# A two-layer graph kernel: one gathered piece in 64 is fetched by SyncE row by row instead of by GpSimd

## The reference

```python
h = relu(layernorm(x))
xW  = einsum('nd,rde->nre', h, W_rel)               # 8 products per node: a table of 100,000 rows of 128
agg = segment_sum(xW[src, edge_type], dst)          # first gather, 212,500 rows of 512 bytes
h2  = gelu(layernorm(agg + h @ W_self + b_conv))    # then a dense feed-forward part
x   = x + (h + h2) + ff(h + h2)
g   = relu(layernorm(x))
xt  = g @ W.T + bias                                # plus 4 source scores per node: a table of rows of 132
alpha = leaky_relu(alpha_src[src] + alpha_dst[dst])
w     = exp(alpha - segment_max(alpha, dst)[dst])
out   = x + segment_sum(xt[src] * w, dst) / segment_sum(w, dst)   # second gather, rows of 528 bytes
```

## Time and profile before

| | us |
|---|---|
| runs | 6048.98, 6045.95, 5961.02 |
| median | 6045.95 |
| span of the profiled execution | 4509.7 |
| median less that span | 1536.3 |
| POOL busy, of the span | 3197.0 |
| indirect transfers of the first and of the second stage | 1680 and 1664 |

### The profile page before, as it was taken

The page is one execution under the profiler, slowest core; times in us unless marked ns, Lnnn a source line. Parts: engine busy times, 40 slices in busy tenths (PEclk is TensorE's granted clock), DMA queues, the critical chain, the costliest instruction groups (busy, mean ns, idle before and its releaser), DMA issues.

```text
span 4509.7 us, 47117 instructions
## 1 busy us (share of the span) xinstructions
PE 2498.0 (55%) x13797; PEld 2093.8 (46%) x13902; DVE 2470.8 (55%) x6772; ACT 962.3 (21%) x3200; POOL 3197.0 (71%) x3372
## 2 busy tenths in 40 slices
PE   7823444444444444444444666666666666666665
PEld 3423343433434333343333556555555565555555
DVE  6741333333333333333334777777777777777777
ACT  4500111111111111111122222222222222222222
POOL 1077777777777777777756777777777777777774
PEclk9966766667667666666666787777777777777777
DMA  8712222222222222222213222222222222222221
GB/s 281 273 50 53 58 62 58 62 58 60 60 58 62 58 60 60 58 62 58 60 43 107 55 57 60 57 57 60 57 60 57 58 60 57 60 57 59 58 57 44
DMA packets 170560, 314.19 MB, mean 70 GB/s; under 512 B 58980, under 2 KB 100108, under 8 KB 169615
## 3 DMA queue, kind: packets, MB, share of 16 engines
q0 software_dynamic: 107008, 222.77, 20.6%
q1 hardware_dynamic: 47810, 81.58, 5.1%
q10 hardware_dynamic: 15490, 6.87, 0.6%
HBM read 239.51 MB, written 71.49 MB: 69 GB/s over the span
## 4 chain that ended last, share of the span: by engine, by line
POOL 68%; issue 23%; PE 6%; DVE 2%; ACT 0%; DMA 0%; POOLq 0%; DVEq 0%; ACTq 0%; SPq 0%
POOL G L512 68%; PE quad L1440 1%; PE quad L1441 1%; PE bank L1440 1%; PE bank L1441 1%; PE bank L1482 0%; PE quad L1511 0%; PE quad L1517 0%; ACT A L663 0%; POOLq L111 0%; PE quad L1434 0%; PE quad L1506 0%; DMA x_res<-in_x 0%; DMA xt_table<-w_all 0%; PE bank L1434 0%
## 5 line engine op out<-in xcount | busy, mean ns | idle before, releaser
L512 POOL DMA_INDIRECT G<-rel_table,idx x1680 | 1601.5, 953 | 705.6 <-issue 511.2
L512 POOL DMA_INDIRECT G<-xt_table,idx x1664 | 1574.6, 946 | 543.8 <-issue 543.8
L1602 PEld LDWEIGHTS quad<-ident,top 128*128 128x128 f32 x3328 | 591.1, 279 | 265.6 <-issue 265.5
L1602 PE MATMUL quad<-ident,top 128*128 128x128 f32 x3328 | 607.6, 367 | 177.5 <-DVEq L1238 177.5
L1025 DVE SCALAR_TENSOR_TENSOR agg<-bank,sel,agg 128x128 f32 x208 | 63.6, 347 | 1093.0 <-PE bank L1482 1091.6
L1633 PE MATMUL bank<-M,onehot 128*128 128x132 f32 x3328 | 432.7, 284 | 149.8 <-DVE M L1287 145.4
L1482 PE MATMUL bank<-G,onehot 128*128 128x128 f32 x1664 | 271.6, 340 | 401.3 <-DMA G<-rel_table,idx 397.0
L1633 PEld LDWEIGHTS bank<-M,onehot 128*128 128x128 f32 x3328 | 398.5, 193 | 181.6 <-issue 181.6
L1482 PEld LDWEIGHTS bank<-G,onehot 128*128 128x128 f32 x1664 | 267.6, 256 | 406.0 <-issue 406.0
L1618 PE MATMUL bank<-Z,w_all 128*128 128x8 f32 x832 | 160.5, 321 | 380.3 <-issue 374.4
L768 ACT ACTIVATE M<-G,M 128x32 f32<-128x32 f32 x1664 | 363.9, 308 | 13.6 <-ACT M L763 0.4
(11 more groups left out here) (320 smaller groups left out, 3530.9 us busy)
## 6 DMA issues: line engine op xcount, KB each, us to landing
rel_table<-G SPq DMA_DIRECT2D x98, 512.0 KB, 3.1
G<-rel_table,idx POOLq DMA_INDIRECT x1680, 2.5
G<-xt_table,idx POOLq DMA_INDIRECT x1664, 7.1
xt_table<-w_all SPq DMA_DIRECT2D x25, 264.0 KB, 3.2
x_mid<-X SPq DMA_DIRECT2D x25, 256.0 KB, 2.0
out<-A SPq DMA_DIRECT2D x24, 256.0 KB
x_res<-in_x ACTq DMA_DIRECT2D x12, 448.0 KB, 5.0
x_res<-x_mid SPq DMA_DIRECT2D x3, 1792.0 KB, 15.5
```

The lines of the kernel that those rows point to most:

```text
L512: g.indirect_dma_start(out=G[:, s, c, 0:width], out_offset=None, in_=table, in_offset=bass.IndirectOffsetOnAxis(ap=idx[:, s, c:c + 1], axi ...
L1602: ins = t.matmul(banks[j][:, hd * P:(hd + 1) * P], top[:, j, hd:hd + 1].to_broadcast([P, P]), ident[:, :], start=False, stop=(hd == HEADS ...
```

## The change

- `SIDES` is the list of groups 3, 7, 11, ... 99: 25 of the 103. For these, in both gather stages, GpSimd issues 15 transfers instead of 16. All of them use slot 3 of `G`.
- SyncE fetches the 16th piece of these groups (`SIDE_C`) into one of three buffers of a new tile `side`. GpSimd prepares the row numbers once in `side_idx`, edge by edge along a partition. For each side piece SyncE does 32 times: load 4 row numbers to registers, then start 4 transfers of one row each (512 bytes in the first stage, 528 in the second) from the table's row to one partition of `side`. A buffer is refilled when its former group has been summed (`agg_done`, or `tail_ready` in the second stage).
- TensorE, in `add_edges`, takes piece 15 of such a group from `side`, behind a wait on the 128 rows. In the second stage VectorE waits for the rows and copies the four score columns of the side piece into `G` ahead of the scores, and ScalarE scales the messages out of `side`.
- The stores of quads to `x_mid`, `xt_table` and `out` move from SyncE to ScalarE (`store_mid`, `store_xt`, `store_done`), but for the last ones, which SyncE still issues behind its side rows.
- Counts of landed transfers become `landed_by(g)`, since slot 3 now gets 15 pieces in these groups.

```diff
+SIDE_C = CHUNKS - 1
+SIDES = [g for g in range(3, MAIN - 3, 4)]
+SIDE_BUFS = 3
+LOADED = 4
+def landed_by(g):
+    return 16 * sum(CHUNKS - (x in SIDES) for x in range(g % SLOTS, g + 1, SLOTS))
...
+            def side_rows(k, g, table, width):
+                for lo in range(0, P, LOADED):
+                    _, rows_of = nc.values_load_multi_w_load_instructions(
+                        side_idx[g:g + 1, k, lo:lo + LOADED], engines=[mybir.EngineType.SP], min_val=0, max_val=table.shape[0] - 1,
+                        skip_runtime_bounds_check_because="the transfer checks its address against the table")
+                    for p, row in enumerate(rows_of, lo):
+                        sp.dma_start(side[p:p + 1, side_of(g), 0:width], table[bass.ds(row, 1), :]).then_inc(side_ready[k][side_of(g)], 16)
+            sp.wait_ge(side_set, 2)
+            for j, g in enumerate(SIDES):
+                if j >= SIDE_BUFS:
+                    sp.wait_ge(agg_done, SIDES[j - SIDE_BUFS] + 1)
+                side_rows(0, g, rel_table, D)
...
-            store_quad(0, first_of(0))
-            sp.wait_ge(s_mid, 16)
-            sp.wait_ge(s_xt, 16)
-            for n in range(1, AHEAD):
-                store_quad(n, first_of(n))
+            store_quad(AHEAD - 1, first_of(AHEAD - 1))
...
-            store_out(0, first_of(0), A)
-            for n in range(1, AHEAD):
-                store_out(n, first_of(n), A)
+            for j, g in enumerate(SIDES):
+                if j >= SIDE_BUFS:
+                    sp.wait_ge(groups.tail_ready, SIDES[j - SIDE_BUFS] + 1)
+                side_rows(1, g, xt_table, XT)
+            store_out(AHEAD - 1, first_of(AHEAD - 1), A)
...
+            g.tensor_copy(side_idx[0:GROUPS, 1, :], by_chunk(src_raw, SIDE_C)).then_inc(side_set, 1)
+            pool.wait_ge(side_set, 1)
...
+            g.tensor_copy(side_idx[0:GROUPS, 0, :], by_chunk(key_flat, SIDE_C)).then_inc(side_set, 1)
...
-                gather(rel_table, s, D, gathered[0][s])
+                gather(rel_table, s, D, gathered[0][s], SIDE_C if gr in SIDES else CHUNKS)
...
-                gather(xt_table, s, XT, gathered[1][s])
+                gather(xt_table, s, XT, gathered[1][s], SIDE_C if gr in SIDES else CHUNKS)
...
             def quad_scalar(n, lo, last, own):
+                if own and n:
+                    store_xt(n - 1)
                 if not last:
                     idx_of(n, 0)
...
                 if not last:
                     idx_of(n, 3)
+                    store_mid(n)
                 third_norm(n)
...
+                    own = kind is groups and c == SIDE_C and n in SIDES
+                    rows_in = side[:, side_of(n), :] if own else G[:, s, c, :]
...
+                    if s == 1 and i >= LAG:
+                        store_done(i - LAG)
...
+                if g in SIDES:
+                    dve.wait_ge(*side_landed(1, g))
+                    dve_stop(dve)
+                    v.tensor_copy(G[:, s, SIDE_C, D:XT], side[:, side_of(g), D:XT]).then_inc(side_taken, 1)
+                    dve.wait_ge(side_taken, SIDES.index(g) + 1)
...
+                    if c == SIDE_C and g in SIDES:
+                        pe.wait_ge(*side_landed(0, g))
+                        pe_stop(pe)
+                        rows_in = side[:, side_of(g), 0:D]
```

More of the change, by code:

```diff
@@ L222, in build @@
         onehot = sb("onehot", [P, CHUNKS, P])
+        side = sb("side", [P, SIDE_BUFS, XT])
+        side_idx = sb("side_idx", [P, 2, P], i32)
         M = sb("M", [P, CHUNKS, HEADS, HD])
@@ L319, in build @@
         gathered = [[sem(f"gathered{k}_{i}") for i in range(SLOTS)] for k in range(2)]
+        side_set, side_taken = sem("side_set"), sem("side_taken")
+        side_ready = [[sem(f"side_ready{k}_{i}") for i in range(SIDE_BUFS)] for k in range(2)]
         oh_ready, agg_done, c_group = (sem(n) for n in ("oh_ready", "agg_done", "c_group"))
@@ L508, in _, with gather @@
                             pattern=[[-1, P]], channel_multiplier=1).then_inc(s_pool, 1)
-            def gather(table, s, width, done):
-                for c in range(CHUNKS):
+            def gather(table, s, width, done, chunks=CHUNKS):
+                for c in range(chunks):
                     g.indirect_dma_start(out=G[:, s, c, 0:width], out_offset=None, in_=table,
@@ L689, in forward, with store_mid, store_xt @@
                     a.activation(hid[:, c % 2, :], banks[1 + c % 2][:, :], ACT.Gelu, bias=b1col[:, c:c + 1]).then_inc(up_sb, 1)
+            def store_mid(n):
+                act.wait_ge(mid_ready, n + 1)
+                act.dma_start(x_mid[:, first_of(n):first_of(n) + QUAD, :], X[:, :, :]).then_inc(s_mid, 16)
+            def store_xt(n):
+                act.wait_ge(xt_sb, n + 1)
+                act.dma_start(xt_table.rearrange("(b p) k -> p b k", p=P)[:, first_of(n):first_of(n) + QUAD, :], xt_sbuf[:, :, :]).then_inc(s_xt, 16)
             def third_norm(n):
@@ L1228, in prepare, with scores @@
                 assert c.n - c0 == STEPS["prep"]
-            def scores(kind, c, s, k, landed):
+            def scores(kind, c, s, k, landed, g=None):
                 c0 = c.n
                 dve.wait_ge(*landed)
+                if g in SIDES:
[3 more added lines that the diff above has]
+                    dve.wait_ge(side_taken, SIDES.index(g) + 1)
                 dve_stop(dve)
@@ L1355, in _ @@
                 prepare(groups, c, row_of(nkey_all, gr), row_of(run_all, gr), gr % 2)
-            scores(groups, c, 0, 0, (gathered[1][0], 16 * CHUNKS))
+            scores(groups, c, 0, 0, (gathered[1][0], landed_by(0)), 0)
             assert c.n == START
@@ L1377, in round_of @@
                 if landed:
-                    scores(groups, c, (s + 1) % SLOTS, 1 - k, landed)
+                    scores(groups, c, (s + 1) % SLOTS, 1 - k, landed, gr + 1)
                 edges(groups, c, gr, s, k, (lambda: merge(groups, c, gr - 1, gr - 1, last, 1 - k)) if last is not None else (lambda: None))
@@ L1382, in _ @@
             c = at(0)
-            round_of(c, 0, 0, 0, first, None, (gathered[1][1], 16 * CHUNKS))
+            round_of(c, 0, 0, 0, first, None, (gathered[1][1], landed_by(1)))
             prepare(groups, c, row_of(nkey_all, 2), row_of(run_all, 2), 0)
@@ L1393, in four_rounds @@
                     round_of(c, gr, (s + 1) % SLOTS, (s + 1) % 2, first, last,
-                             (gathered[1][(s + 2) % SLOTS], i * (16 * CHUNKS) + 16 * CHUNKS * (1 + (s + 2) // SLOTS)), done if s == 1 else None)
+                             (gathered[1][(s + 2) % SLOTS], landed_by(gr + 1)), done if s == 1 else None)
                     prepare(groups, c, row_of(nkey_all, gr + 2), row_of(run_all, gr + 2), (s + 1) % 2)
@@ L1494, in _ @@
             pe.wait_ge(s_setdve, 6)
[L1495 to L1499, removed]
+            for g in range(2, LAG * SLOTS):
+                add_group(g)
             def flip(done, count):
@@ L1574, in quad_tensor @@
                 for s in range(1, SLOTS - 1):
-                    add_edges(g + s, s, s % 2, landed(s))
+                    add_group(g + s)
                 forward(n)
@@ L1579, in quad_tensor @@
                 else:
-                    add_edges(g + SLOTS - 1, SLOTS - 1, 1, landed(SLOTS - 1))
+                    add_group(g + SLOTS - 1)
                 project(n)
```

33 lines of the change are left out of this document (22 added, 11 removed).

## The result

| | before | after | ratio |
|---|---|---|---|
| the measured comparison | 6047.47 us (5961.02 to 6050.14) | 7179.33 us (7159.59 to 7194.86) | 1.1905 [1.181, 1.200] |
| span of the profiled execution | 4509.7 | 7169.5, of a run of 7171.19 | |

The change makes the kernel 19% slower. The forecast was 5984 us, no change beyond 2%. The first thing to see is in the last row: after the change the span and the time of the same run are 2 us apart. Nothing like 1536 us lies outside of this span.

A forecast was written before the change was run, and what follows sets the result against it. GpSimd's indirect transfers were taken to bound both gather stages. Removing 50 of 1.25 us saves 62.5 us, all else costing nothing: 6046 − 62.5 = 5984 us, with 5895 to 6200 as the range for 8 in 10.

The forecast's parts named there:

- 1536 us: Gap between the traced span before and the runs' median, 1536.3 us, taken as outside the span and carried over unchanged.
- Rival 2: SyncE's side rows become the bound in both gather stages, from 0.615 us a row: 6366 to about 7000 us; chance 0.18.
- GpSimd sets the pace, in both stages: Both gather stages run at GpSimd's 1.25 us per indirect transfer, 80.0 us per four groups.
- Rival 4: The part outside the span grows with the program's instruction count: 6669 us if all of it does; chance 0.05.
- Removal, 62.5 us: GpSimd loses one indirect transfer in 25 groups of each gather stage: 50 × 1.25 us = 62.5 us gained.
- A row on SyncE, 0.545 us: Address 0.165, transfer 0.29 and load 0.09 us per side row: 69.8 us a piece, under GpSimd's 78.75 per four groups.
- the upper bound of 0.745: One side row on SyncE with transfer and load at their dear end: 0.745 us, 95 us a piece.
- The other edits at nothing: Stores moved to ScalarE, row-number copies on GpSimd, the score copy on VectorE and new waits: hidden, costed at nothing.
- Rival 1: Each row transfer on SyncE costs as much as a wide one, 0.36 us: 5985 to 6050; chance 0.15 with Rival 3.
- Rival 3: Contention from 3200 more small transfers per stage lengthens GpSimd's step by 0.019 us: 6046; chance 0.15 with Rival 1.

The follow-up runs named there:

- before_fourth: The kernel before, unedited, run again for a trace of the long kind: 6070.71 us, span 6068.9.
- half_sides_again: Changed kernel with side pieces only in every eighth group, 13 a stage instead of 25, in long runs: 6065.74 us against 6069.74 before, ratio 0.9992.
- one_transfer: Changed kernel with each side piece fetched by one transfer of 128 fixed (wrong) rows, in short runs: 4447.69 us, ratio 0.9861 to the kernel before.
- stores_moved: Changed kernel with an empty list of side groups, so essentially only the stores move to ScalarE, in long runs: 6048.89 us against 6054.91 before, ratio 0.9995.

## Why the prediction was wrong

**Where the 1132 us come from.** In the long kind, the first stage grew from 2834.2 − 216.6 = 2617.6 us to 3422.7 (214.0 to 3636.7), the second from 3130.4 to 3426.5 (3675.1 to 7101.6): 805 + 296 = 1101 us, all of the 1100.6 between the spans 6068.9 and 7169.5. Rival 2's formula with the paces of this kind, 25 × (133.4 − 99.7) + 25 × (135.8 − 120.4), gives 843 + 385 = 1228: the right size, and 127 too much. Why it is too much stays open.

The steps in their order:

1. *"GpSimd sets the pace, in both stages"*: right in the trace that was read, false in the runs to be forecast. There four groups take 99.7 and 120.4 us.
2. *The 1536.3 us were carried over unchanged.* This is the step that failed. They were not outside of the span: before_fourth has a run of 6070.71 with a span of 6068.9. The trace of before and the runs of before were of two kinds, and all prices came from the short one. A median 34% above the span was put down as a constant instead of as a sign that the prices do not belong to these runs. Rival 4 was the only case in which this part could change, and it was sized by the number of instructions in the program, which half_sides_again refutes.
3. *Removal, 62.5 us*: right in short runs (61.7 with a free SyncE, 59.3 for the change as it is).
4. *A row on SyncE, 0.545 us*: in short runs 0.576, and 5 us of lead in each four groups instead of 9. The address and the row were 0.415 (forecast 0.455), the load of four with its gap 0.60 us, so 0.15 a row instead of the 0.09 taken. The sum came near by luck in part, since the two errors offset each other. In the long runs it was 133.4 / 128 = 1.04 us, beyond the upper bound of 0.745, which had been made from rows of the other kind. This is where step 2 did its harm: the price of a row is the term that turned a gain into a loss.
5. *The other edits at nothing*: right in both kinds (one_transfer in short runs, stores_moved in long ones). The side copy on VectorE took 0.16 to 0.27 us in short runs and 0.17 in long ones, inside the bounds of nothing and 0.6.
6. *The rivals.* Rival 1 (a row at the price of a wide transfer) did not occur: 225 ns. Rival 2 is what happened, with all the signs named for it: TensorE and VectorE wait for `side`, GpSimd idles ahead of the fourth group (in the first stage 25 times, 1124 us), SyncE's queue has hardly a wait left. Its cause was none of those given (a dear row, a slow load) but the slots. Its chance of 0.18 rested on short prices. Rival 3 did not occur: GpSimd's transfer took 944 ns in short runs and 947 in long ones, before and after the change. Rival 4's sign (a short span with a high median) did not show.

The Trainium skill (DMA: Bandwidth & Descriptors, "Latency and other measured facts") was set aside in step 4 for the two loads of 277 and 280 ns. The 1600 loads of four numbers took 563 ns in the middle, close to its 600. The row worked out from it, 0.615 us, was no nearer to the 0.576 measured than the forecast's 0.545, since the row without its load cost less than either sum had it.

**What stays open.** What makes a run one kind or the other, and what the slots are. Each comparison ran on one chip, so chip and occasion are not told apart. The slots begin and end with GpSimd's gathering. In the trace of the changed kernel SyncE falls into them mostly 3 to 6 us after GpSimd has begun to issue without a pause and leaves them 2 to 5 us after it stops, and nearly all of SyncE's and TensorE's slots lie in these stretches, which are 64% of the span; in before_fourth TensorE's do. ScalarE, VectorE and GpSimd keep their busy time (962.3, 2470.8 and 3197.0 us in the short trace of before, 964.8, 2466.8 and 3197.8 in the long one). In the traces of long runs many records of semaphores are missing (23,000 to 29,000 where short ones have 69,000 to 81,000), which may be why some of their waits stand as "issue" or "remote". The Trainium skill (NOTIFIC — the notification-queue block, "Overflow: three behaviours, one of which stalls the engine") says that a full queue of records can stall the engine that makes them. Slots of one 0.70 us at the start and one at the end of an instruction would fit that, but every run here was recorded and none of the traces shows such a queue, so it is only argued. If it is so, the slots, and the 19% with them, belong to the recording of the runs and not to the kernel alone.

## What to carry to other kernels

Compare the span of the trace with the time of the runs before pricing anything: where they differ by much more than the 2 us seen here, the trace is of other conditions, and a new load on a queue wants a margin for them. A margin of 6% (a piece of 73.7 us for a pace of 78.75) did not hold when each instruction got dearer (134 us for a pace of 100 to 120), while the variants with half the pieces or with 128 instead of 416 instructions a piece lost nothing; so keep the number of instructions low, and not just their time, on a queue that others wait for. That the number counts is shown for runs with slots only; in the short ones the time did.

## What was not expected of the hardware

- The same program took about 4509 us on two chips and about 6050 on two others, with nothing between 4594 and 5961.
- In the long kind an instruction of SyncE or TensorE often takes 1.40 us in the stretches in which GpSimd gathers, a register operation like a matrix product, while the indirect transfers of GpSimd beside it stay at 1.25 us a step.
- A load of four numbers to registers takes 0.563 us, one of a single number 0.50 in the middle (274 to 919 ns).
- A transfer of one row of 512 bytes takes SyncE 0.225 us with its address in a register (0.255 where each row has a load of its own) and 0.252 with a fixed one, and 6400 of them cost GpSimd's transfers nothing.
